# Routed adapters in split fp32: TensorE takes tiles 2 to 31 in pairs, with two PSUM banks in turn

## The reference

```python
def _L0_cond_ref(x, weight, adapter_ids):
    w = weight[adapter_ids]
    return jnp.einsum('bsi,boi->bso', x, w)
x = x + _L0_cond_ref(x, L0_cond_weight, itok_B_3_7)
```

## Time and profile before

| what | value |
|---|---|
| median of 3 runs | 107.21 us (106.95 to 107.35) |
| the profiled execution: its time | 106.78 us |
| its span, first to last instruction | 105.2 us |
| TensorE busy | 99.8 us, 95% of the span |
| ScalarE busy | 56.0 us, 53% |
| VectorE busy | 52.9 us, 50% |
| GpSimd busy | 42.7 us, 41% |
| DMA | 22.92 MB, mean 218 GB/s |

### The profile page before, as it was taken

How to read it: one execution, slowest core, us unless ns; L and a number is a source line. 1 busy time by engine, 2 the same in 40 slices (tenths; PEclk the granted TensorE clock), 3 DMA queues, 4 the chain that set the end, 5 groups by cost and what they waited for, 6 DMA issues and landing times.

```text
span 105.2 us, 2286 instructions
## 1 busy us (share of the span) xinstructions
PE 99.8 (95%) x440; PEld 80.1 (76%) x440; DVE 52.9 (50%) x107; ACT 56.0 (53%) x103; POOL 42.7 (41%) x58
## 2 busy tenths in 40 slices
PE   5998999999999999999999999999999999999960
PEld 2665688888888888888888888888888888888830
DVE  1556985595076820785178617853673179220000
ACT  5075207496249922595269745944866459342220
POOL 6543702507530772047404870474263324433000
PEclk9999999999999999999999999999999999999999
DMA  0976689958996999689975688476637654542333
GB/s 12 304 184 179 168 201 341 317 160 319 374 341 205 283 340 383 189 202 376 345 242 144 221 245 284 136 218 208 192 117 232 217 170 117 192 153 100 106 100 100
DMA packets 24944, 22.92 MB, mean 218 GB/s; under 512 B 3121, under 2 KB 20018, under 8 KB 24930
## 3 DMA queue, kind: packets, MB, share of 16 engines
q1 hardware_dynamic: 19298, 9.45, 33.2%
q0 software_dynamic: 2608, 8.06, 20.7%
q10 hardware_dynamic: 3024, 5.24, 15.7%
HBM read 17.30 MB, written 8.91 MB: 249 GB/s over the span
## 4 chain that ended last, share of the span: by engine, by line
PE 87%; DMA 4%; issue 2%; ACT 2%; POOL 1%; POOLq 1%
PE out_ps L523 87%; DMA w_raw<-in_weight 4%; POOL w_raw L176 1%; ACT w_hi L337 1%; ACT out_tile L344 1%; POOLq L179 1%; ACT L297 0%; PE rank_ps L561 0%; POOLq L156 0%
## 5 line engine op out<-in xcount | busy, mean ns | idle before, releaser
L287 POOL DMA_INDIRECT out<-out_tile,row_of x31 | 35.2, 1137 | 48.1 <-ACT out_tile L344 42.9
L523 PE MATMUL out_ps<-w_hi,xt_hi 128*128 (+1 forms) x136 | 53.2, 391 | 0.3 <-ACT w_hi L337 0.3
L523 PE MATMUL out_ps<-w_lo,xt_hi 128*128 (+1 forms) x136 | 53.0, 390 | 0.0
L439 DVE TENSOR_TENSOR xt_lo<-x_raw,xt_hi 128x512 fp32r<-128x512 f32 x34 | 23.5, 692 | 30.0 <-ACT xt_hi L315 28.8
L523 PE MATMUL out_ps<-w_hi,xt_lo 128*128 (+1 forms) x136 | 36.5, 389 | 0.0
L315 ACT ACTIVATE xt_hi<-x_raw 128x512 fp32r<-128x512 f32 (+1 forms) x35 | 21.4, 614 | 18.3 <-DMA x_raw<-in_x 16.3
L523 PEld LDWEIGHTS out_ps<-w_hi,xt_hi 128*128 128x128 f32 x136 | 25.5, 188 | 6.3 <-ACT w_hi L337 0.7
L523 PEld LDWEIGHTS out_ps<-w_lo,xt_hi 128*128 128x128 f32 x136 | 25.5, 188 | 5.6 <-DVE w_lo L434 0.4
L523 PEld LDWEIGHTS out_ps<-w_hi,xt_lo 128*128 128x128 f32 x136 | 25.5, 188 | 5.2
L344 ACT ACTIVATE out_tile<-out_ps 128x512 f32<-128x512 f32 x34 | 20.1, 590 | 13.1 <-PE out_ps L523 13.1
L337 ACT ACTIVATE w_hi<-w_raw 128x512 fp32r<-128x512 f32 x32 | 18.4, 622 | 13.8 <-DVE w_raw L176 9.1
(11 more groups left out here) (60 smaller groups left out, 10.4 us busy)
## 6 DMA issues: line engine op xcount, KB each, us to landing
x_raw<-in_x SPq DMA_DIRECT2D x130, 64.0 KB, 3.2
w_raw<-in_weight ACTq DMA_DIRECT2D x6, 1024.0 KB
w_raw<-in_weight ACTq DMA_DIRECT2D x6, 256.0 KB, 4.4
w_raw<-in_weight SPq DMA_DIRECT2D x2, 256.0 KB, 3.9
out<-out_tile,row_of POOLq DMA_INDIRECT x31, 4.1
out<-out_tile ACTq DMA_DIRECT2D x6, 64.0 KB, 1.9
out<-out_tile SPq DMA_DIRECT2D x6, 64.0 KB, 1.9
x_raw<-in_x POOLq DMA_DIRECT2D x4, 64.0 KB, 2.4
```

The costliest lines, as they stand in the source:

```text
L287: nc.gpsimd.indirect_dma_start(out=out_rows, out_offset=bass.IndirectOffsetOnAxis(ap=row_of[:, t:t + 1], axis=0), in_=out_tile[n][:, :], i ...
L439: nc.vector.tensor_tensor(xt_lo[t % XT_BUFS][:, :, :, :], x_raw[t % X_BUFS][:, :, :, :].rearrange("p m c r -> p c m r"), xt_hi[t % XT_BUFS ...
L523: return nc.tensor.matmul(out_ps[n][:, :], lefts[left][k][:, c, :, :].rearrange("p m r -> p (m r)"), rights[right][:, bass.ds(rank, 1), c, ...
```

## The change

TensorE's loop over tiles 2 to 31 now takes two tiles at once. `multiply(t, ranks)` waits for all that both tiles need and then alternates: a matmul for tile t into its bank, the same one for tile t+1 into the next bank. The number of matmuls, their operands and the order of the sum within a tile stay as they were. Tiles 0, 1 and those from 32 on are done one at a time as before. `product_ready` is counted up at the 23rd and the 24th matmul of a pair. `NEEDED_FROM` moves ranks 2, 3 and 4 one tile ahead.

```diff
-NEEDED_FROM = (0, 2, 7, 11, 15, 20, 24, 28)
+NEEDED_FROM = (0, 2, 6, 10, 14, 20, 24, 28)
...
-                if t >= OUT_BANKS:
-                    pe.wait_ge(out_copied, t - OUT_BANKS + 1)
-                elif t == OUT_BANKS - 1:
+            def multiply(t, ranks):
+
+                end = t + len(ranks)
+                if end > OUT_BANKS:
+                    pe.wait_ge(out_copied, end - OUT_BANKS)
+                elif end == OUT_BANKS:
                     pe.wait_ge(ranks_ready, 1)
-                pe.wait_ge(w_lo_ready, rank * CHUNKS + CHUNKS)
-                pe.wait_ge(x_hi_ready, t + 1)
+                for rank in ranks:
+                    pe.wait_ge(w_lo_ready, rank * CHUNKS + CHUNKS)
+                pe.wait_ge(x_hi_ready, end)
                 for c in range(CHUNKS):
-                    product("hi", "hi", c, c == 0, False)
-                    product("hi", "lo", c, False, False)
-                pe.wait_ge(x_lo_ready, t + 1)
+                    for right in ("hi", "lo"):
+                        for i, rank in enumerate(ranks):
+                            product(t + i, rank, "hi", right, c, c == 0 and right == "hi", False)
+                pe.wait_ge(x_lo_ready, end)
                 for c in range(CHUNKS):
-                    last = product("lo", "hi", c, False, c == CHUNKS - 1)
-                last.then_inc(product_ready, 1)
+                    for i, rank in enumerate(ranks):
+                        last = product(t + i, rank, "lo", "hi", c, False, c == CHUNKS - 1)
+                        if c == CHUNKS - 1:
+                            last.then_inc(product_ready, 1)
...
-                multiply(t, 0)
+                multiply(t, (0,))
             pe.wait_ge(tables_ready, 1)
-            for t in range(FIRST_TILES, MIN_TILES):
-                multiply(t, rank_of(t))
+            for t in range(FIRST_TILES, MIN_TILES, PAIR):
+                multiply(t, (rank_of(t), rank_of(t + 1)))
```

More of the change, by code:

```diff
@@ L515, in _ @@
             keep_warm(WARM_UPS[3])
[L517 to L539, removed]
-                    last.then_inc(product_ready, 1)
-                    return
-                if t >= OUT_BANKS:
-                    pe.wait_ge(out_copied, t - OUT_BANKS + 1)
-                elif t == OUT_BANKS - 1:
@@ new lines, in _, with product @@
+            lefts, rights = {"hi": xt_hi, "lo": xt_lo}, {"hi": w_hi, "lo": w_lo}
+            def product(t, rank, left, right, c, start, stop):
+                return nc.tensor.matmul(out_ps[t % OUT_BANKS][:, :],
+                                        lefts[left][t % XT_BUFS][:, c, :, :].rearrange("p m r -> p (m r)"),
+                                        rights[right][:, bass.ds(rank, 1), c, :].rearrange("p a o -> p (a o)"),
+                                        start=start, stop=stop)
@@ new lines, in multiply_first @@
+            def multiply_first():
+                for i, (left, right, c) in enumerate(FIRST_ORDER):
+                    if right == "lo":
+                        pe.wait_ge(w_lo_ready, c + 1)
+                    elif left == "hi":
+                        pe.wait_ge(w_hi_ready, c + 1)
+                        if c == 0:
+                            pe.wait_ge(x0_half_ready, 1)
+                        elif c == CHUNKS // 2:
+                            pe.wait_ge(x_hi_ready, 1)
+                    elif c == 0:
+                        pe.wait_ge(x_lo_ready, 1)
+                    last = product(0, 0, left, right, c, i == 0, i == len(FIRST_ORDER) - 1)
+                last.then_inc(product_ready, 1)
@@ L554, in multiply @@
-                last.then_inc(product_ready, 1)
+                    for i, rank in enumerate(ranks):
+                        last = product(t + i, rank, "lo", "hi", c, False, c == CHUNKS - 1)
+                        if c == CHUNKS - 1:
+                            last.then_inc(product_ready, 1)
             def rank_of(t):
                 return pe.value_load(rank_of_tile[0:1, t:t + 1], min_val=0, max_val=ADAPTERS - 1)
-            multiply(0, 0)
+            multiply_first()
             pe.wait_ge(slots_ready, 2)
@@ L571, in _ @@
                 with conditional(pe, t, tiles):
-                    multiply(t, rank_of(t))
+                    multiply(t, (rank_of(t),))
 def kernel(**inputs):
```

## The result

The changed kernel takes 110.41 us at the median of six runs (109.33 to 111.35), the kernel before 107.12 (106.95 to 107.35): the ratio is 1.0295, with a 95% interval of 1.0255 to 1.0335. That is slower, as forecast, and inside the range of 108.7 to 110.8, but 1.1 us above the point and above the 108.9 to 109.8 that the forecast gave for itself. The profiled execution is the fastest of the six, 109.33 us with a span of 107.7, against 106.78 and 105.2 before.

What follows compares the result with a forecast made beforehand. TensorE, busy 95% of the span without idle time, was taken as the bound. A 2.05 us stall at the first pair plus 0.05 at tile 9 gave 107.21 + 2.1 = 109.3 us, range 108.7 to 110.8.

Steps and rivals of the forecast that it cites:

- a second stall: Rival: tile 9 late or ACT's chain over 10.88 us, adding up to 1.5 us: 109.8 to 110.9 us; 15%.
- What bounds the kernel: TensorE, busy 95% of the span, steps of 0.2267 us, no idle time; any stall before it is paid in full.
- The banks in turn: TensorE's steps between matmuls: alternating banks gains 0, at most 4.8 us; rival that the change is faster, 10%.
- Back-to-back issue gap: Skill page's 0.2158 us per matmul of 512 columns; would give back 3.9 us if the single bank made the difference.
- The wait for the second tile: At pair 2 and 3, TensorE waits for tile 3's xt_hi, starting at 16.35 instead of 14.30: a 2.05 us stall.
- The step from the event to the matmul: From xt_hi ready through the sequencer's register instruction to TensorE's matmul: 0.15 us, between 0.03 and 0.3.
- so it ends at 16.20: Tile 3's xt_hi on ACT starts at 15.57 after its load and takes 0.63 us; work ahead of it unchanged.
- The other pairs: Pairs after 2 and 3: cost 0 from ACT's chain, 0.05 us in the sum for a late load at tile 9.
- ACT's chain: Copies and splits from a pair's end, ready at 10.19 before 10.88 us: 0.69 us of cover, cost 0.
- my 0 to 0.3: Pair 8 and 9: tile 9's xt_hi meets its due time by 0.02 us; stall 0 to 0.3 us, 0.05 in the sum.
- The clock: Rival: the granted clock falls behind TensorE's 2 us stall, costing 3.1 us, up to 112.4 us; 5%.
- A second HAM failure mode: psum-queue depth-cycling: Skill page's case of cycling PSUM banks making TensorE idle and its clock oscillate; no more than the clock rival's 5%.

Runs made afterwards that it cites:

- the run with pairs from tile 6: Changed kernel with ranks in the kernel before's order, tiles 2 to 5 singly, pairs and alternating banks from tile 6 on: 108.06 us, ratio 1.0088.
- the stall filled: Changed kernel with 14 warm-up matmuls ahead of pair 2 and 3: 109.84 us; the same with the kernel before's ranks: 109.70 us.
- in series: Changed kernel with common waits kept, but the two tiles of a pair done one after the other, banks not alternating: 109.57 us, ratio 1.0243.
- wait alone: Kernel before, tiles singly, with one change: tile 2 waits for the xt_hi of tile 3; 110.09 us.
- old order: Changed kernel with the ranks of the kernel before (2, 3 and 4 not a tile ahead): 111.35 us.
- new order alone: Kernel before, tiles singly, with ranks 2, 3 and 4 moved a tile ahead: 106.90 us, ratio 1.0004.
- the pairs in series from tile 6: Changed kernel with the kernel before's ranks, tiles 2 to 5 singly, then pairs with common waits but no bank alternation: 108.19 us, ratio 1.0018.
- the stall of 1.15 us: Changed kernel with the kernel before's ranks and rank 1's four loads issued behind the splits of tiles 2 and 3: 109.00 us, ratio 1.0192.

## Why the prediction was right, and where its size was off

**What was right, and what was luck.** The sign was right, for the reason given: no gain from the banks, and a stall at the first pair. The point was 1.1 us low. The range reached up to 110.8 for a second stall, which the changed kernel's profile doesn't have; what filled it were falls of the clock, most of which I had left outside it, and as far as the runs tell later landings of tile 3's load, which I had not priced. That the median, with the fall in three of six runs, still lies 0.4 us inside is luck in that part.

**What bounds the kernel: right.** TensorE has no idle time to give back, and the stall went into the span whole: behind the first matmul all executions whose clock stayed agree within 0.2 us, but for the one that stood 0.3 us for tile 9.

**The banks in turn, worth 0: right, and shown.** 0.2271 us a step in the changed kernel and in the run with pairs from tile 6, against 0.2267. The figure of the Trainium skill ("TensorE: Matmul & The Clock Gate", "Back-to-back issue gap"), 0.2158 us, is reached by neither; the rows at the tile's end had told that the single bank wasn't what separates the two. What does is left open.

**The wait for the second tile: right in mechanism, and 0.1 us short in the one profiled execution.** 2.15 us were measured for 2.05. The step from the event to the matmul, for which I took 0.15 us between 0.03 and 0.3, is 0.25 to 0.33 over the seven profiles, and 0.25 in five of them.

**The term that was mis-sized is when tile 3's xt_hi is ready, "so it ends at 16.20".** I took it from one execution and held that nothing ahead of it changes. That is true of the program, but not of the landing: over the profiles of the changed kernel and of the nine that load as it does, the split starts between 14.86 and 16.27. Before, tile 3 was wanted at 17.02, and its split was over at 16.90 even in the latest of these (17.15 with the 0.25 us to the matmul), so all but 0.13 us of this scatter was covered. The common wait takes all cover away, and each tenth of a late landing is a tenth of the time, as the table shows. My bounds of 1.9 to 2.2 us for the stall held only the sequencer's share. The runs at full clock, 109.33 to 110.04, fit a first matmul of up to 17.3; that is worked out from their spans, not seen.

**The other pairs: right in the profile, but on average not free.** Tile 9's split ended at 32.52, as worked out at 32.50, and ACT's chain held in every weight pair. (In the profile with the stall filled tile 9 cost 0.3 us, the upper end of my 0 to 0.3.) But the pairs from tile 6 on cost about 1 us at the median with and without the turn of the banks. Two traces show a pair that stands: for a late load, in series, which tiles done singly would have covered, and for some 0.1 us at tile 6 for ACT's chain, with the alternation. That late loads are the cause in the other runs is argued and not shown. I had put a second stall at 15%, as a rival that happens or doesn't; it seems to be a part of most runs, and of different size in each.

**The clock: a rival at 5% that happened in half of the runs.** I priced it at up to 3.1 us from the warm-up; one fall costs 1.4 to 1.6. Taking the four kernels with an unfilled stall of full length at tile 2 (changed, wait alone, in series, old order), 13 of 26 runs have a mean clock of 0.985 or less; the two with the stall filled have 0 of 12, and the two kernels without any common wait (new order alone, and before) none. That the fill prevents the falls at tile 2 is thus shown by the counts. A stall at tile 2 isn't the only way to one: the pairs in series from tile 6 have it in two of nine runs, and with the stall of 1.15 us it came in one of six. One fall seen in a trace came 2.1 us into an idle time of 2.4, the other one matmul behind an idle time of 2.5, and the changed kernel's profiled 2.0 us had none. Length alone doesn't decide: behind the 3.3 us at tile 8 the clock stayed. The trace before had no idle time over 0.3 us behind the warm-up, and that no fall is in it said nothing of what 2 us would do. This was the faulty reasoning: the absence of a case was taken for evidence on it.

The rule of the Trainium skill's same page, "TensorE: Matmul & The Clock Gate" ("A second HAM failure mode: psum-queue depth-cycling") isn't what acted here: the wait alone has the falls with no more changes of bank than before, and 312 alternating steps ran at a clock of 1.00.

**The sum, then.** The six runs of the changed kernel have a mean of 110.38 us. 107.1 + 2.2 (what the profiled execution has more than the median before) + 0.8 (1.6 in half of the runs) are 110.1. The 0.3 us that are left fit landings later than the profiled one, as in the table, and late loads of later pairs; how they divide isn't settled.

## What to carry to other kernels

Cover that a profile shows is spent by an execution that it doesn't show: before a wait is moved ahead of a transfer, price it with the transfer's landings over several executions, and count every consumer that moves. If an engine at full rate gets a new idle time, cost the clock behind it as well; half of the changed kernel's runs paid some 1.6 us for it here, and fourteen small matmuls in the gap avoided that. Whether two banks in turn help can be read before trying it, at the places where the kernel changes bank anyway.

## What the hardware did that I had not expected

The granted clock fell to half for some eight matmuls at a stall of 2.4 to 2.5 us, once when TensorE was already at work again, and in some executions and not in others of the same program. The split that waits for tile 3's load of 256 KB, issued by the same code from 9.96 to 10.31 us on, moved by 1.4 us between executions (14.86 to 16.27). That is more than three times the 0.4 us by which the first six runs of the kernel before differed, where it is covered. The kernel before isn't always that still, though: of its 45 later runs eight took more than 107.4 us, up to 109.41, at mean clocks of 0.996 or more; none of these was profiled.
